# Layer 0's q turned by DMA as two 16-bit float pieces, normed ahead of the turn, and projected three tiles ahead

## The reference, cut to what matters

```
def _L0_xattn_ref(latents, context, Wq, Wk, Wv, Wo, q_norm_w, k_norm_w):
    kv = jnp.concatenate([context, latents], axis=1)
    q = (latents @ Wq)...; k = (kv @ Wk)...; v = (kv @ Wv)...
    q = rms_norm(q, q_norm_w); k = rms_norm(k, k_norm_w)
    scores = jnp.einsum('bhgqd,bhkd->bhgqk', qg, k) * scale
    probs = softmax(scores); out = einsum(probs, v)
    return out @ Wo
x = x + tanh(g_xattn[0]) * _L0_xattn_ref(_layernorm(x), ctx_4096, ...)
x = x + tanh(g_ffn[0])   * _L0_ffn_ref(_layernorm(x), ...)      # low-rank experts
x = x + tanh(g_xattn[1]) * _L1_xattn_ref(_layernorm(x), ctx_4096, ...)   # no rms_norm
x = x + tanh(g_ffn[1])   * _L1_ffn_ref(_layernorm(x), ...)      # gated, 1792 wide
```

## Time and profile before

| what | value |
|---|---|
| median of 3 runs | 1331.15 us (1329.89 to 1333.68) |
| profiled execution, its own time | 1332.94 us |
| its span in the trace | 1331.1 us |
| granted TensorE clock, mean | 0.994 |
| tiles of layer 0, of layer 1 | 64, 32 |

### The profile page before, as it was taken

How to read it: one execution, slowest core, us unless ns; L and a number is a source line. 1 busy time by engine, 2 the same in 40 slices (tenths; PEclk the granted TensorE clock), 3 DMA queues, 4 the chain that set the end, 5 groups by cost and what they waited for, 6 DMA issues and landing times.

```text
span 1331.1 us, 24159 instructions
## 1 busy us (share of the span) xinstructions
PE 1295.2 (97%) x7776; PEld 1138.5 (86%) x7776; DVE 994.8 (75%) x2463; ACT 745.6 (56%) x2511; POOL 521.9 (39%) x829
## 2 busy tenths in 40 slices
PE   7999999999999999999999999899999999989998
PEld 6888888888888888888888988788989989878886
DVE  6788777877777877787787788878777788863433
ACT  5556655665565665566557665566666666632221
POOL 2545544544544554454355442322433233540000
PEclk9999999999999999999999999999999999999999
DMA  6333243232332332331433331343442424370000
GB/s 198 64 88 68 60 96 65 63 80 63 76 82 61 72 89 48 79 92 35 95 79 61 72 56 33 52 80 69 92 99 50 96 55 102 66 171 4 32 0 32
DMA packets 236656, 95.76 MB, mean 72 GB/s; under 512 B 204944, under 2 KB 222864, under 8 KB 236560
## 3 DMA queue, kind: packets, MB, share of 16 engines
q1 hardware_dynamic: 210416, 58.75, 23.2%
q10 hardware_dynamic: 22160, 29.64, 7.4%
q0 software_dynamic: 3984, 6.29, 2.0%
HBM read 39.08 MB, written 2.10 MB: 31 GB/s over the span
## 4 chain that ended last, share of the span: by engine, by line
PE 73%; DVE 14%; ACT 4%; issue 4%; POOL 3%; DMA 1%; DVEq 0%; ACTq 0%; POOLq 0%
PE bank L494 19%; PE bank L496 19%; PE bank L495 19%; PE bank L707 7%; DVE split L1054 4%; PE bank L723 4%; PE bank L571 3%; DVE mx L1128 2%; DVE pieces L1163 2%; ACT split L758 2%; PE bank L563 1%; ACT scratch L813 1%; POOL split L1398 1%; DVE scratch L1101 1%; DVE pieces L1153 1%
## 5 line engine op out<-in xcount | busy, mean ns | idle before, releaser
L494 PE MATMUL bank<-split 128*128 128x256 f32 (+6 forms) x2120 | 711.8, 336 | 14.4 <-DVE split L1054 7.9
L496 PE MATMUL bank<-split 128*128 128x256 f32 (+6 forms) x2120 | 693.0, 327 | 0.0
L495 PE MATMUL bank<-split 128*128 128x256 f32 (+6 forms) x2120 | 692.1, 326 | 0.0
L494 PEld LDWEIGHTS bank<-split 128*128 128x128 f32 (+2 forms) x2120 | 402.4, 190 | 49.3 <-DVE split L1054 8.1
L496 PEld LDWEIGHTS bank<-split 128*128 128x128 f32 (+2 forms) x2120 | 401.9, 190 | 35.7
L495 PEld LDWEIGHTS bank<-split 128*128 128x128 f32 (+2 forms) x2120 | 403.1, 190 | 27.2
L1425 POOL CAST split<-turned 128x512 fp32r<-128x512 f16 x384 | 228.0, 623 | 289.2 <-DMA turned<-pieces 288.4
L758 ACT ACTIVATE split<-bank 128x512 fp32r<-128x512 f32 (+7 forms) x456 | 194.0, 449 | 214.0 <-PE bank L571 176.1
L1054 DVE TENSOR_TENSOR split<-bank,split 128x512 fp32r<-128x512 f32 (+7 forms) x456 | 224.5, 503 | 45.8 <-ACT split L758 38.6
L1128 DVE TENSOR_REDUCE mx<-bank 128x2 f32<-128x512 f32 x192 | 131.7, 686 | 83.5 <-PE bank L496 81.7
L1163 DVE SCALAR_TENSOR_TENSOR pieces<-scratch,rs,pieces 128x256 f16<-128x256 f32 x384 | 180.9, 512 | 6.2 <-ACT pieces L825 4.0
(11 more groups left out here) (73 smaller groups left out, 1206.4 us busy)
## 6 DMA issues: line engine op xcount, KB each, us to landing
raw<-in_wq_a ACTq DMA_DIRECT2D x14, 512.0 KB, 3.7
raw<-in_wo_a ACTq DMA_DIRECT2D x14, 512.0 KB, 3.4
raw<-in_wkv_a ACTq DMA_DIRECT2D x7, 512.0 KB, 3.4
turned<-pieces SPq DMA_TRANSPOSE x192, 3.1
raw<-in_wq_c ACTq DMA_DIRECT2D x8, 384.0 KB, 3.3
raw<-in_wo_c ACTq DMA_DIRECT2D x4, 512.0 KB, 3.6
split<-in_down_t POOLq DMA_DIRECT2D x2, 1024.0 KB, 5.6
x<-in_x SPq DMA_DIRECT2D x1, 1536.0 KB, 13.1
```

What stands on the lines that cost most here:

```text
L494: pe.matmul(out, whi, mhi, start=start, stop=False)
L495: pe.matmul(out, whi, mlo, start=False, stop=False)
L496: return pe.matmul(out, wlo, mhi, start=False, stop=stop)
```

## The change

Only layer 0's q path, the place of q in the steps of both layers, and who makes the high pieces of the probabilities are changed.

- In layer 0 ACT squares q straight from bank 6, POOL makes `rq` (now scaled by 2^15), ACT writes the high 16-bit piece of q times `rq` (`q_high`) and DVE the low one (`q_low`), four rows each, into the space of `qn`. SP turns both pieces by one DMA into the first half of `turned` (`turn_q`), and POOL casts them into `qT` (`cast_q`, two rows). `q_evac`, `q_turn`, `qt_evac` and `qt_low` are gone in layer 0. The exponentials have no scale any more, and the row maximum is negated where it is taken, so L1133 and L1136 are gone.
- `q_proj` in step b is that of tile b+3, in both layers. It waits until `q_low` of the tile before is done, since bank 6 is held until then. The load and the split of a new group's q weights come one step earlier, and the load of its k and v weights after them.
- In all of layer 0 ACT makes the high pieces of the probabilities.
- POOL does `k_norm` after the cast of the second half of tile b, no longer before it, and `cast_q` behind that.
- The first half of the pieces may be turned only when q of the next tile has been cast, and `turn_q` of tile n only when the first half of tile n-2 has been cast: both use the same half of `turned`.
- Before the loop, three q tiles are projected, and `scores` of tile 0 come after all of them.

```diff
+            def turn_q(n):
+                s = attn[L0.name]
+                sp.wait_ge(s.qb_done, NH * n + NH)
+                if n >= 2:
+                    sp.wait_ge(s.cast_done[0], 2 * (n - 1))
+                elif n == 1:
+                    sp.wait_ge(s.qcast_done, 2)
+                sp.dma_start_transpose(q_turned, q_halves).then_inc(s.qturned, 16)
...
+                    if i == 0 and L is L0:
+                        sp.wait_ge(s.qcast_done, 2 * min(n + 2, L0.tiles))
                     sp.dma_start_transpose(turned_in[:, i], halves[:, i, :]).then_inc(s.turned[i], 16)
...
@@ tensor, step
-            if two is not None:
-                q_proj(*two)
-                k_turn(*two)
+            if three is not None:
+                q_proj(*three)
+            if two is not None:
+                k_turn(*two)
...
-            if two is not None:
-                q_turn(*two)
+            if three is not None and three[0] is L1:
+                q_turn(*three)
@@ scalar
+            def q_high(L, g, b):
+                act.wait_ge(s.rq_done, count(g, b, 1, 1))
+                if not starts(g, b):
+                    act.wait_ge(s.qturned, count(g, b, 16, 0))
+                for h in range(NH):
+                    r = NH * (b % 2) + h
+                    act.activation(q_piece[:, 0, h, :], bank[6][:, h * P:(h + 1) * P], ACT.Copy,
+                                   scale=rq[:, r:r + 1]).then_inc(s.qa_done, 1)
@@ vector
+            def q_low(L, g, b):
+                dve.wait_ge(s.qa_done, count(g, b, NH, NH))
+                for h in range(NH):
+                    r = NH * (b % 2) + h
+                    dve.scalar_tensor_tensor(q_piece[:, 1, h, :], bank[6][:, h * P:(h + 1) * P], rq[:, r:r + 1],
+                                             q_piece[:, 0, h, :], ALU.mult, ALU.subtract).then_inc(s.qb_done, 1)
@@ gpsimd, step
-            if two is not None and two[0].normed:
+            cast_probs(L, g, b, 1)
+            if two is not None and two[0] is L0:
                 k_norm(*two)
-            cast_probs(L, g, b, 1)
+                cast_q(*two)
...
-            if two is not None and two[0].normed:
-                q_norm(*two)
+            if three is not None and three[0] is L0:
+                q_norm(*three)
```

More of the change, by code:

```diff
@@ L641, in step @@
                 beside_norm, lora, second = beside(L, g, b)
-                one, two, prev = later(L, g, b, 1), later(L, g, b, 2), earlier(L, g, b)
+                one, two, three, prev = (later(L, g, b, n) for n in (1, 2, 3, -1))
                 if two is not None:
@@ L677, in _ @@
             k_turn(L0, 0, 0)
-            q_turn(L0, 0, 0)
-            scores(L0, 0, 0)
             norm_turn(0, 2)
@@ L683, in _ @@
             k_turn(L0, 0, 1)
-            q_turn(L0, 0, 1)
+            norm_turn(0, 3)
+            q_proj(L0, 0, 2)
+            scores(L0, 0, 0)
             def gate_up(n):
@@ L870, in step @@
                 beside_norm, lora, second = beside(L, g, b)
-                one, two = later(L, g, b, 1), later(L, g, b, 2)
-                new_kvq = later(L, g, NT - 1, 1) if b == NT - 3 else None
+                one, two, three = (later(L, g, b, n) for n in (1, 2, 3))
+                new_kv = later(L, g, NT - 1, 1) if b == NT - 3 else None
+                new_q = later(L, g, NT - 1, 1) if b == NT - 4 else None
                 new_o = b == 1 and not is_at(L, g, L0, 0)
@@ L1251, in step @@
                 if one is not None:
[L1252 to L1256 removed]
+                    probs_low(*one, 0)
+                if three is not None and three[0] is L0:
+                    if one is not None:
+                        probs_low(*one, 1)
+                    if two is not None:
+                        k_low(*two)
+                else:
+                    if two is not None:
+                        k_low(*two)
+                    if one is not None:
+                        probs_low(*one, 1)
                 if lora is not None:
@@ L1264, in step @@
                     lora_add(lora)
-                if two is not None:
-                    qt_low(*two)
+                if three is not None and three[0] is L0:
+                    q_low(*three)
+                if three is not None and three[0] is L1:
+                    qt_low(*three)
                 if next_norm is not None:
@@ L1521, in _ @@
             k_norm(L0, 0, 1)
-            o_lo(L0, 0, 0)
-            o_lo(L0, 0, 1)
+            norm_rstd(0, 3)
+            cast_q(L0, 0, 0)
             q_norm(L0, 0, 1)
-            o_lo(L0, 0, 2)
-            o_lo(L0, 0, 3)
+            q_norm(L0, 0, 2)
+            cast_q(L0, 0, 1)
+            for c in range(L0.oc):
+                o_lo(L0, 0, c)
             cast_probs(L0, 0, 0, 0)
```

264 lines of the change are left out of this document (140 added, 124 removed).

## The result

The changed kernel takes 1338.24 us (median of 17 runs, 1335.08 to 1340.73) against 1331.15 (17 runs) before: ratio 1.0049, 95% interval 1.0041 to 1.0058. It is half a per cent slower, where 0.9% faster was forecast, and above the forecast's range. The profiled execution took 1337.59 us, with a span of 1335.7 and a mean granted clock of 0.987 (before 1331.1 and 0.994).

What follows compares the result with a forecast made beforehand. TensorE's own work was taken to bound layer 0's step. Start +8.1, steps -22.4, borders +4.2, q turns -1.3, group 7 +2.0 and end -2.1 sum to -11.5 us: 1331.15 to 1319.7, said as 1320, range 1308 to 1335.

Steps and rivals of the forecast that it cites:

- What leaves TensorE, 0.44 us a step: Layer 0's steps: without `q_turn`'s four transposes a step falls from 11.90 to 11.46 us, 11.40 without border waits.
- The ring of 10.35 us: Layer 0's chain from `row_max` over `q_norm` to `q_low` and `o_low`: 10.35 us, under the step's 11.4.
- The first rival: Layer 0's ring sets the step: about 1339 us at 11.84, 1328 at 11.6; slower overall had 0.17.
- the fourth: Rival: the step's third DMA slows the others, so turns and casts come late; part of rival 1, no own chance.
- The borders, 0.7 us a group: Step 5 of groups: TensorE waits for k's scaling and q's second low part; net 0.7 at six borders, 4.2 us.
- The start, +8.1 us at step 6: Before the loop: tile 0's scores behind three q projections make `k_turn` 12.3 us late at step 0, 8.1 at step 6.
- The end, −1.4 in all after step 57: After step 57: three q turns gone -1.3, group 7 +2.0, the q projection done ahead -2.1 us.
- Group 7: Layer 0's last group: POOL's splits of expert weights push `q_norm` back by some 4 us once, costing +2.0 us.
- The q projection done ahead: One more q projection done at `k_turn` comes back: 0.65 at layer 1's handover, up to 2.1 in the tail; -2.1 us.
- The sum: Whole kernel: all terms total -11.5 us against the profiled 1332.94, giving 1321.4; against the median 1319.7, said as 1320.
- the second rival: Start (12) and borders (2.5 more each) eat the gain: +4, 1335 us, or 1332 with borders at 2.0; same had 0.13.

Runs made afterwards that it cites:

- the one with k first: Changed kernel with k's high and low parts ahead of the second pair of pieces on ScalarE and VectorE in layer 0: 1333.96 us, ratio 1.0019 to before.
- the kernel with the new start: Changed kernel with tile 0's scores ahead of the third q projection and group 0's output-weight low parts on VectorE: 1330.95 us, ratio 0.9994 to before.
- the last experiment: Changed kernel with k's parts, k_norm, q's weight low parts, the start reordered, and k's and v's weight low parts ahead of cast_q: 1318.64 us, ratio 0.9904 to before.

## Why the prediction was wrong, point by point

**What leaves TensorE, 0.44 us a step: right.** Ordinary steps are 11.39 to 11.41 apart, 11.40 forecast.

**The ring of 10.35 us: right.** It measures 10.3 (the forecast's terms add up to 10.33), with all its terms near: VectorE's four rows of q 1.13 (1.15 forecast), ScalarE's pieces 1.71 (1.6), its four rows of q 1.14 (0.9), its wait for `rq` 1.49 (1.4). The first rival fell. So did the fourth: the pieces' turns still land in 3.2 us (median; 3.1 before), by the page's part on DMA issues (and q's stay hidden, since no wait of TensorE leads to them in an ordinary step):

```profile
turned<-pieces SPq DMA_TRANSPOSE x192, 3.2
```

**The borders, 0.7 us a group: the failed step.** Two errors lie in it. At step 5 the place and the cause were right (the second low part of q's weights, then k's scaling), but the step lost 1.6 us, against 1.0 forecast: GpSimd's own rows stretch there too, the cast at 397.45 to 1.63 us and the low part at 399.05 to 1.71 from 1.30. Larger is what the forecast put at nothing, without a reason: steps 2 and 6 lose 0.6 to 1.0 and 0.5 to 0.8. k's low part stands behind both halves now, as the order of rows said, and I priced the four low pieces at the unhurried 0.87 a pair, though GpSimd's three low parts run beside them in every step 2. The trace of before had the warning: 2.36 us for 0.61 at 343.83, beside the same low parts. That the stretched row is the cause in step 2 is shown by the kernel without the output weights' low parts; that its place matters in both steps, by the one with k first. The steps of a group take 2.98 us more than eight ordinary ones, against 0.54 before: 2.44 net, where 0.7 was forecast. Over 51 steps the lag fell by 7.8 us where the forecast had 18.2.

**The start, +8.1 us at step 6: the other failed step.** It came to +16.6. The order of things was right: the maxima of tile 0 began at 43.5, 42.4 forecast. Then the low pieces took 2.56 us instead of 1.7, beside GpSimd's low parts of the output weights; GpSimd's two rows for a layer norm (53.22 to 54.06), which the forecast didn't have, stood between the casts of the two halves; `k_norm` behind the casts ended at 56.2, 53.5 forecast, and `k_turn` of step 0 came 2.8 late. From there to step 6 another 5.7 us were lost: 2.2 in step 1, 2.0 in step 5 (the border, which I had left out of group 0's step 5), and 1.5 spread over the others. The lower granted clock, 0.87 and 0.96 up to 60 and 130 us, where it was 0.94 and 1.00, is part of the 16.6; how large a part was not measured by itself. An estimate from these shares (0.07 of 60 and 0.04 of 70 us) puts it at 7.0 us at most. The start's new order was worth 7.0 us at step 6, its higher clock included. `k_norm`'s place was worth 3.1 at a clock of 0.83 and 1.00, which by the same estimate differs by 0.4 us in all, so that is the order's.

**The end, −1.4 in all after step 57: it was −4.1.** Group 7 cost nothing on balance (lag 8.8 to 8.2). In layer 1 the lag fell by 2.7 at step 78 and by 0.4 at step 79, because before had a stall there that the change doesn't have; that its earlier loads and splits took it away was not tested. I had not looked at layer 1's steps one by one. TensorE's timeline of before:

```profile
988.50 0.50 PE L494 MATMUL bank<-split 128*128 128x384 f32 x1 [1.92 <-POOL split L1398]
991.36 0.63 PE L563 MATMUL bank<-ident,scratch 128*96 128x128 f32 x2
```

The step that ends there takes 13.67 us, the one ahead of it 10.29; after, it is 10.97. The q projection done ahead came back: step 93, which has none any more, takes 9.05 us in place of 10.91. From there to the end the lag grows by 1.8 again. The wait of 3.60 us at 1175.75 isn't the reason, since before had one of 3.01 in the same place:

```profile
1172.03 0.66 PE L520 MATMUL bank<-ident,scratch 128*128 128x128 f32 x4 [3.01 <-DVE scratch L1076]
```

The loss goes with the clock instead, 0.90 from 1150 to 1200 us where it was 0.97. From `k_turn` of step 93 to the end the changed kernel takes 184.1 us, and before 182.4; the kernel with the new start, which has the same program there as the change and a clock of 0.97, takes 181.8. What lowered the clock in the one and not in the other was not found.

**The sum.** Against the profiled execution the forecast was −11.5 and the outcome 1337.59 − 1332.94 = +4.65, a miss of 16.2: +8.5 in the start, +10.4 in the borders up to step 57, −2.7 behind them. It is the second rival's mechanism, start and borders, with the start larger than it had (16.6, not 12) and the borders as it had them (2.44 net; it had 2.5). Its +4 meets the measured +4.65 in part by luck: 4.6 more in the start and 3.7 less behind step 57 nearly cancel. I held against it that the step behind a border recovers; it did not, since my times for it came from the queues' order alone, as if every row kept its duration.

The second part of the change, the high pieces on ScalarE, was right to keep apart: alone it gains 3.4 us, and without it the changed kernel loses 12 more.

## What to carry to other kernels

When a step is shortened, price the exceptional steps (start, borders of groups, layers) one by one, each from its own rows of before, since a gain of 0.44 us in 51 steps is paid away by 2.4 us in each of 6 groups and one slow start. Rows of two engines that fall together don't keep the durations they have apart, so look in the trace of before for the longest duration of a row as well as for the usual one, and an operand that the bound engine waits for goes ahead of long rows that nobody waits for as soon. In these in-order queues a row moved to the front mostly made another one late: follow the wait until somebody has room, as the last experiment did.

## What the runs showed that I had not expected

- VectorE's row with two inputs from SBUF (128x256, 16-bit out) doubles beside GpSimd's two-input rows: four in 3.53 us for 1.68. A row with one input stretches too: a pair in 2.53 us for 0.61, and in the kernel before in 2.36.
- GpSimd's rows stretch as well, beside VectorE's own low parts: two casts 1.63 us in place of 1.17, a low part 1.71 in place of 1.30.
- Four transposes in TensorE's stream cost 0.44 us, 0.11 each, as the steps of 11.84 and 11.40 show; the rows' own durations say 0.60.
